# The last loops of a six-stage kernel written out on all five engines, and its stages closed without GpSimd's own drain

## The reference

```python
h = _layernorm(x) * (1 + ca) + sa
x = x + ga * _L0_attn_ref(h, ...)     # causal softmax attention, 16 heads of 16 channels, keys gated
h = _layernorm(x) * (1 + cb) + sb
x = x + gb * _L0_ffn_ref(h, ...)      # shared SwiGLU network + 8 experts, 2 of them per token
h = _layernorm(x) * (1 + ca) + sa
x = x + ga * _L1_attn_ref(h, ...)     # delta rule in chunks of 32 tokens, 4 heads of 64 channels
h = _layernorm(x) * (1 + cb) + sb
x = x + gb * _L1_ffn_ref(h, ...)      # linear layer on rows quantised to int8
```

```python
attn = qi @ jnp.swapaxes(ki, -1, -2) * tril_inc
u_t = ui - wi @ S
o_i = qi @ S + attn @ u_t
S_new = g[..., None, None] * S + jnp.einsum('bhck,bhcv->bhkv', ki, u_t)
```

## Time and profile before

| | |
|---|---|
| median of 3 runs | 2902.31 us (2901.59 to 2902.42) |
| profiled execution | 2902.24 us |
| its span, from the first to the last instruction | 2900.4 us |
| instructions | 88193 |
| mean granted clock of TensorE | 0.942 of full speed |
| busy share of the span: PE, PEld, DVE, ACT, POOL | 90%, 54%, 78%, 56%, 7% |
| data moved by DMA | 133.19 MB, mean 46 GB/s |
| ends of the stages setup, project, attention, layer0_out, layer1_front, recurrence | 33, 208, 1743, 2168, 2509, 2900 us of the span |

### The profile page before, as it was taken

The page is one execution under the profiler, slowest core; times in us unless marked ns, Lnnn a source line. Parts: engine busy times, 40 slices in busy tenths (PEclk is TensorE's granted clock), DMA queues, the critical chain, the costliest instruction groups (busy, mean ns, idle before and its releaser), DMA issues. The chain is left out here.

```text
span 2900.4 us, 88193 instructions
## 1 busy us (share of the span) xinstructions
PE 2617.9 (90%) x36424; PEld 1573.6 (54%) x36424; DVE 2259.8 (78%) x4398; ACT 1627.7 (56%) x2406; POOL 199.6 (7%) x228
## 2 busy tenths in 40 slices
PE   6889999999999999999999998999988998128996
PEld 3332566665666655665566524555545666116774
DVE  3559899999999998999999824565556999775887
ACT  2330677777777777777777791111116777216673
POOL 1238000000000000000000000000000000100000
PEclk8995899999999999999999998999998999659998
DMA  4234011011110111101110001000000333313441
GB/s 145 86 100 83 3 28 29 5 27 27 28 29 5 27 28 28 28 6 27 28 29 7 4 20 52 14 29 15 14 8 13 97 102 103 119 37 106 124 120 58
DMA packets 158639, 133.19 MB, mean 46 GB/s; under 512 B 103097, under 2 KB 135995, under 8 KB 153275
## 3 DMA queue, kind: packets, MB, share of 16 engines
q1 hardware_dynamic: 152571, 124.08, 17.8%
q10 hardware_dynamic: 4224, 4.19, 0.4%
q0 software_dynamic: 1536, 0.40, 0.1%
HBM read 79.98 MB, written 46.66 MB: 44 GB/s over the span
## 5 line engine op out<-in xcount | busy, mean ns | idle before, releaser
L709 DVE TENSOR_REDUCE attn_pm<-attn_MS 128x1 f32<-128x512 f32 (+3 forms) x2304 | 1331.7, 639 | 112.3 <-PE attn_MS L753 94.8
L695 ACT ACTIVATE attn_PT<-attn_ES 128x1024 f32<-128x1024 f32 (+5 forms) x1152 | 1040.7, 951 | 389.0 <-PE attn_ES L788 385.1
L803 PE MATMUL attn_OP<-attn_PT,attn_VH 128*17 128x512 f32 (+2 forms) x4608 | 638.8, 557 | 0.4 <-issue 0.3
L753 PE MATMUL attn_MS<-head_KX,head_QX 96*32 96x512 bf16 (+12 forms) x3456 | 397.2, 393 | 4.4 <-DVE attn_pm L709 3.5
L753 PE MATMUL attn_MS<-attn_KX,attn_QX 96*32 96x512 bf16 (+7 forms) x2880 | 317.0, 364 | 2.4 <-issue 1.1
L753 PE MATMUL attn_MS<-after_attention,attn_QX 96*32 96x512 bf16 (+7 forms) x2880 | 309.2, 358 | 1.5 <-DVE attn_pm L709 1.0
L788 PE MATMUL attn_ES<-head_QX,head_KX 99*32 99x512 bf16 (+6 forms) x3456 | 283.2, 360 | 7.8 <-ACT attn_PT L695 4.4
L788 PE MATMUL attn_ES<-attn_QX,after_attention 99*32 99x512 bf16 (+10 forms) x2880 | 241.8, 357 | 1.7 <-DMA attn_QX<-attn_parts 1.3
L788 PE MATMUL attn_ES<-attn_QX,attn_KX 99*32 99x512 bf16 (+8 forms) x2880 | 237.7, 357 | 0.0
L1189 PE MATMUL l0out_ring<-l0out_w,l0out_sT 128*128 128x512 f32 x512 | 224.9, 592 | 0.0
L753 PEld LDWEIGHTS attn_MS<-head_KX,head_QX 96*32 96x32 bf16 x3456 | 140.7, 97 | 135.6 <-DVE attn_pm L709 62.8
(11 more groups left out here) (295 smaller groups left out, 3341.2 us busy)
## 6 DMA issues: line engine op xcount, KB each, us to landing
vk_beta<-front_vk SPq DMA_DIRECT2D x8, 1024.0 KB, 4.0
kq_transposed<-l0out_w_in SPq DMA_DIRECT2D x8, 1024.0 KB, 4.8
delta_VK<-vk_beta SPq DMA_DIRECT2D x32, 256.0 KB, 2.8
delta_QK<-kq_transposed SPq DMA_DIRECT2D x32, 256.0 KB, 2.9
attn_QX<-qk_parts SPq DMA_DIRECT2D x60, 128.0 KB, 7.7
after_attention<-attn_out SPq DMA_DIRECT2D x18, 256.0 KB
x_res<-in_L_attn_x_dram ACTq DMA_DIRECT2D x8, 512.0 KB, 8.0
qk_parts<-project_hi SPq DMA_DIRECT2D x8, 512.0 KB, 2.9
```

The source lines that it names most:

```text
L695: nc.scalar.activation(PT[u % NPT][:, 512 - wa:512 + wb], ES[half][:, 512 - wa:512 + wb], ACT.Exp, scale=DH ** -0.5).then_inc(exp_done, 1)
L709: nc.vector.tensor_reduce(pm[r][:, i, c:c + 1], MS[slot][:, 0:w], AX.X, ALU.max).then_inc(max_taken, 1)
L753: last = nc.tensor.matmul(MS[slot][r, 0:seen], QX[b][0:ROWS, i * P + 32 * g:i * P + 32 * g + 32], KX[b][0:ROWS, 512 * c:512 * c + seen], s ...
L803: last = nc.tensor.matmul(OP[32 * j:32 * j + DH + 1, 512 - w:512], VH[b][:, kt, :], PT[(2 * n + half) % NPT][:, o:o + w], start=(kt == 0), ...
```

## The change

Two edits, each made throughout:

1. Every `Fori` becomes a Python `range` with the same bounds: 21 loops, on all five engines, in `project`, `attention` (SyncE's alone), `layer0_out`, `layer1_front` and `recurrence`. Every instruction of every turn is then in the program once for each turn, with constants as wait values and addresses. Branches, and the register operations that served the loops, are gone. The steps, their order on each engine, the buffers and the waits are the same.
2. The six blocks are opened with `nc.Block(no_gpsimd_drain=True)`.

```diff
-        block = st.enter_context(nc.Block())
+        block = st.enter_context(nc.Block(no_gpsimd_drain=True))
...
-            with sp.Fori(0, G) as g:
+            for g in range(0, G):
                 cols = bass.ds(g * 512, 512)
...
-            with act.Fori(0, G - 1) as g:
+            for g in range(0, G - 1):
                 parts(g, True)
                 modulate(g + 1)
...
-            with pe.Fori(0, G - 1) as g:
+            for g in range(0, G - 1):
                 products(g)
                 turn_over(g + 1)
...
-            with sp.Fori(0, TURNS) as i:
+            for i in range(0, TURNS):
                 for b in range(NB):
                     turn(NB * i + b, b, True)
...
-            with pe.Fori(0, G - 1) as g:
+            for g in range(0, G - 1):
                 network(g)
                 project(g + 1)
                 experts(g, 0)
...
-            with pe.Fori(1, G // 2 - 1) as i:
+            for i in range(1, G // 2 - 1):
                 for b in range(2):
                     turn(2 * i + b, b, True, True, True)
...
-            with sp.Fori(3, NU - 1) as i:
+            for i in range(3, NU - 1):
                 load_pair(i)
                 send(i - 3)
...
-            with act.Fori(2, NU - 1) as i:
+            for i in range(2, NU - 1):
                 turn(i, True, True, True, True)
...
-            with dve.Fori(3, NU - 1) as i:
+            for i in range(3, NU - 1):
                 turn(i, True, True, True, True, True)
...
-            with pe.Fori(3, NU - 1) as i:
+            for i in range(3, NU - 1):
                 turn(i, True, True, True, True, True)
```

More of the change, by code:

```diff
@@ L292, in _ @@
             nc.gpsimd.memset(v17[:, :, :, DH:DH + 1], 1.0).then_inc(pd, 4)
-            with pool.Fori(0, G) as g:
+            for g in range(0, G):
                 for m in range(4):
@@ L353, in _ @@
             normalise(0)
-            with dve.Fori(0, G - 1) as g:
+            for g in range(0, G - 1):
                 for m in range(2):
@@ L970, in load @@
                 first_group.load(sp, q, inv_rows)
-            with sp.Fori(1, G - FIRST) as g:
+            for g in range(1, G - FIRST):
                 load(g, g + FIRST)
-            with sp.Fori(G - FIRST, G) as g:
+            for g in range(G - FIRST, G):
                 load(g, g - (G - FIRST))
@@ L1116, in turn @@
                 experts(g, 3, q)
-            with dve.Fori(0, G - FIRST - 1) as g:
+            for g in range(0, G - FIRST - 1):
                 turn(g, g + FIRST, g + FIRST + 1)
             turn(G - FIRST - 1, G - 1, 0)
-            with dve.Fori(G - FIRST, G - 1) as g:
+            for g in range(G - FIRST, G - 1):
                 turn(g, g - (G - FIRST), g - (G - FIRST) + 1)
@@ L1499, in _ @@
             turn(1, 1, True, True, False)
-            with act.Fori(1, G // 2 - 1) as i:
+            for i in range(1, G // 2 - 1):
                 for b in range(2):
@@ L1691, in _ @@
             turn(2, True, True, True, False, True)
-            with dve.Fori(3, G - 1) as n:
+            for n in range(3, G - 1):
                 turn(n, True, True, True, True, True)
@@ L2019, in _ @@
                 residual_and_bias(n)
-            with pool.Fori(1, NU) as n:
+            for n in range(1, NU):
                 residual_and_bias(n)
```

## The result

The changed kernel takes 2926.26 us (median of 4 runs, 2922.91 to 2932.42) where the kernel before takes 2901.95 (2901.59 to 2902.42): a ratio of 1.0079, with a 95% interval from 1.0066 to 1.0092. It is slower by 24.3 us. The profiled execution took 2928.23 us (span 2926.4), 26.0 us more than that of before. The median lies above the forecast of 2909.4 and above the end of the range, 2920.

What follows compares the result with a forecast made beforehand. PE, busy for 90% of the span, was taken as the limit, with PE and DVE handing over in a ring in the recurrence. 2902.2 - 3.9 (projection) - 3.0 (recurrence hand-overs) + 14.1 (packets) = 2909.4 us; range 2896 to 2920.

Steps and rivals of the forecast that it cites:

- Halts, gross: PE in the recurrence: instruction packets halt it 0.61 us each, 2.6 packets a turn, 1.6 us gross a turn.
- Net cost of the coming packets: Recurrence: fetching PE's written turns costs 1.28 us net for each of 11 turns, +14.1 us (+4 to +21).
- The turns ahead of the loop: Recurrence turns already written out before the loop: given no term in the sum, so taken as unchanged.
- Hand-overs in the recurrence: Without register operations for waits, three hand-overs save 0.25 us a turn over 12 turns: -3.0 us (-1 to -6).
- Projection: Faster hand-overs save 0.43 us a turn over 7 turns, SyncE's last transfers 0.9 us; together -3.9 us (-2 to -5).
- Expert stage: MoE stage: PE is full and 16 matmuls take 7.03 us looped or written; 0, packets covered by long matmuls.
- Front: Front of layer 1: looped and written turns take about the same time; 0, within 1 us.
- Attention: Attention stage: already written out except on SyncE, whose transfers are early; 0.
- Stage ends: Six block ends: GpSimd's drain is over before another engine's last drain starts; 0 each, within 0.2 us.
- A: Rival for the whole kernel: fetching stays hidden and only hand-overs count, -6.9 us, 2895.3 us; chance 0.15.
- B: Rival: each recurrence turn costs what the last written one did, 1.71 us x 11 = 18.8; 2914.1, up to 2921; chance 0.23.
- C: Rival: recurrence halts fall into waits, 0.6 us a turn, +6.6 against -6.9; 2901.9 us, no change; chance 0.15.

Runs made afterwards that it cites:

- e3_all_but_pe_recurrence: The changed kernel with PE's recurrence loop alone put back as a loop; 2907.11 us, ratio 1.0016 to the kernel before.
- e1_drains_only: The kernel before with only the six block lines changed to no_gpsimd_drain=True, every loop kept; 2908.45 us against 2904.05, ratio 1.0017.
- e7_changed_again: The changed kernel run once more, unaltered; 2922.52 us, ratio 1.0058 to the kernel before.
- e5_shifted_by_128: The changed kernel with 64 more transposes (128 instructions) on PE at the recurrence stage's start; 2927.41 us, ratio 1.0082 to the kernel before.
- The filling: 14 unused transposes on PE per projection turn, added to the kernel before with projection and non-PE recurrence loops written out; 2894.70 us, ratio 0.9977.

## Why the prediction was wrong

The mechanism and the place were right, the sign too; the sizes were not. What failed is the sum: it held one loss (14.1 us for packets) against two gains (3.9 and 3.0 us), with the granted clock at nothing in all three and every other stretch at 0. Packets cost 16.8 us, the gains came to 1.3 and 0.8, and the stretches at 0 moved. From the forecast of 7.1 us to the 26.0 us between the two profiled executions 18.9 are missing: 2.7 in the packets, 2.2 in the recurrence's hand-overs, 2.6 in the projection, 4.0 in the turns ahead of the loop, 4.5 in the front, 3.2 in attention, 1.4 in the rest of the recurrence, less 1.7 in the expert stage. Only the recurrence's part comes back in every trace: the stage took 409.0 to 413.1 us in the six in which PE fetches in every turn, and 387.6 to 393.1 in the eight others.

1. *Halts, gross: right.* Forecast 0.61 us a packet and 2.6 packets a turn. The changed kernel has 31 packets in the twelve turns, and PE's halts of over 0.4 us that are put down to issue add up to 15.9 us there, 0.51 a packet. They are 15, and 14 of them end 2.2 to 3.0 us behind the start of a packet, so about half of the packets halt PE and half do not. One packet came within the warm loop of before too, at 2706.5 us, just ahead of the stretch in the earlier trace rows; its turn took 16.40 us like the others.
2. *Net cost of the coming packets: mis-sized.* Forecast 1.28 us for each of 11 turns, 14.1. The twelve turns took 15.9 us more than before (213.6 - 197.7), and 16.8 us more than in e3_all_but_pe_recurrence (196.8), which differs in PE's loop alone; that is what the packets cost net. What is in it and was not in the sum is the granted clock. Two of the twelve turns ran at 0.91 to 0.92 and cost 1.8 us more each, 3.5 together; without them the term is 13.3, close to the forecast. The rows held a hint: the clock in the earlier trace rows is 1.00 in all three turns, and I took from them that halts leave it alone. I named no price and no rival for the clock.
3. *The turns ahead of the loop: left out.* Forecast unchanged; they took 60.8 us against 56.8. But these turns are written out in every kernel, and in the 14 traces of this case they took 54.3 to 60.8 us (the kernel before again 59.5, the changed one again 59.3). So the 4.0 us lie within what they move by themselves, and the 17.55 and 18.11 us, from the second of which I priced a written turn, were one draw from that spread. Here too the clock is in it: i = 1 took 17.55 us at 1.00 and 19.09 at 0.91.
4. *Hand-overs in the recurrence: mis-sized.* Forecast 0.25 us a turn, 3.0 in all; e3_all_but_pe_recurrence shows 0.10 a warm turn, 0.8 over the twelve (197.7 - 196.8, since the first took 17.39 against 17.25), with PE still in registers. PE's own share can't be told from its halts.
5. *Projection: half right.* A turn fell by 0.54 us (20.31 to 19.77), more than the 0.43 forecast from its twin, and SyncE's tail by 0.6 us. But two of the five turns from 104 us on, all at 1.00 before, now started at half clock, 1.7 us each, and the stage gave 0.7 us (1.3 with setup) instead of 3.9. No halt for a packet shows there; the term missing is again the clock. A turn of the changed kernel that kept the clock and one that lost it, as in the earlier trace rows, and the clock over the first 1.72 us of each:

```profile
125.52 7.55 PE L380 MATMUL project_qkp<-project_hT,l0out_w 128*128 128x512 f32 x16 [2.04 <-ACT project_hT L262]
145.28 9.22 PE L380 MATMUL project_qkp<-project_hT,l0out_w 128*128 128x512 f32 x16 [2.04 <-ACT project_hT L262]
...
145.28:147.00 1.72, 1.72 (x2) 0.84 (x3) 0.23 (x1) 0.00 (x0) 0.00 (x0) 0.50 0.71 240
125.52:127.24 1.72, 1.72 (x4) 0.87 (x5) 0.23 (x1) 0.00 (x0) 0.00 (x0) 1.00 0.73 242
```

6. *Expert stage: right.* Turns of 50.77 us in every kernel, and 7.03 us for the 16 matmuls as in the earlier trace rows, with seven packets more on the queue (9 against 2 in that stage). *Front: open.* Its +4.5 us don't come back in the second trace of the changed kernel (341.0), but the stage is over 345 us in four of the seven traces with the written loop and in none of the seven with PE's loop kept, and the forecast had 0 and nothing for the clock. *Attention:* +3.2 us, as much as between the two traces of the kernel before. *Stage ends: right* at the ends themselves; the 4.4 us of e1_drains_only stay unexplained.

Of the rivals, A (fetching stays hidden) holds for the experts and, as far as no halt for a packet shows there, for the projection, and falls in the recurrence. The Trainium skill's rule (Runtime: NRT & Kernel Launch, Instruction fetch mechanics) that straight code is mostly prefetched and full unrolling preferred agrees with the trace where matmuls are long; where weight loads leave every 10 ns or so the halts of 0.45 to 2.54 us go against it. B, 18.8 us on the turns, was nearest in its total, 2914 to 2921, but for a wrong reason: it took one turn's 18.11 us for all, where the turns really differ by their edges. C falls: i = 7 halted for 4.2 us and lost 5.3, of which the clock made 1.8, so 3.5 of the 4.2 were lost. The range was too narrow because each of its terms had the clock at 1.00 and none had the spread of an unchanged stage, which the traces of the kernel before put at 3.4 us for attention alone. That the total came out 24.3 us and not the 18.1 of e7_changed_again (2922.52 against 2904.37) is in part such spread; both lie above 2920.

## What to carry to other kernels

In this kernel writing a loop out cost nothing that shows on engines with long or few instructions. PE, which issues hundreds of small ones in a ring with DVE, was better off with a loop whose body stays loaded: 1350 instructions did and 2700 didn't, and a jump back over the longer body cost 3.5 us by itself. Before pricing a halt, look at the granted clock behind it, and where an engine idles ahead of its bulk of matmuls, try filling the gap.

## What the runs showed of the hardware

- In the two traces of the changed kernel 26 of the 28 halts of over 0.4 us that are put down to issue, within the twelve turns, ended 2.2 to 3.1 us after a packet had started; a packet itself took 0.9 to 1.9 us.
- A branch back over 2700 instructions took PE 3.5 us, one over 1350 at most 0.24.
- After a standstill of 2.5 us within the recurrence TensorE's granted clock was at 0.50 for some 3.4 us, which made 1.8 us; after an equal one in e5_shifted_by_128 it stayed at 1.00. It also fell behind a halt of 1.74 us (i = 12 of the changed kernel, 0.91) and not behind one of 1.68 (the first of i = 7).
- In the projection the written turns with 2.04 us of idle time ahead of `qkp` lost the clock in about every second turn (two of the four that start between 104 and 167 us in the changed kernel). Of the looped ones with 2.23 us none of the 16 in that stretch did, in four traces. The filling shows that the idle time has a part in it. What tells the two apart stays open.
- One kernel's turns keep their lengths from run to run: i = 7 took 21.72, 20.61, 21.19 and 21.14 us in four executions of three kernels. How long an unrolled turn takes can hang on code that was added long before it.
